# Order of two short GpSimd chains in the last stage of a two-layer gated cross-attention kernel

## The reference, cut to what matters

```python
def expert(w1, bb1, gg1, bbe1, w2, bb2, gg2, bbe2):
    h = relu(layernorm(xf @ w1 + bb1, gg1, bbe1))     # first product
    return layernorm(h @ w2 + bb2, gg2, bbe2)         # second product
...
gate_scores = xf @ gate_W + gate_b                    # top 2 of 4, softmax over the two
out = sum(weights[..., None] * exp_out, axis=1)
x = x + tanh(g_ffn[1]) * (out + xf)                   # xf = layernorm(x)
```

## Time and profile before

| what | value |
|---|---|
| median of 3 runs | 2152.01 us |
| the profiled execution's own time | 2150.5 us |
| its span, first to last instruction | 2148.7 us |
| granted TensorE clock, mean over the span | 0.985 |
| PE busy | 2052.7 us (96%) |
| PEld busy | 1790.2 us (83%) |
| DVE busy | 1762.3 us (82%) |
| ACT busy | 1501.9 us (70%) |
| POOL busy | 1220.5 us (57%) |

### The profile page before, as it was taken

One profiled execution on the slowest core, in us unless ns is written; L12 is line 12 of the kernel. 1 busy time (PEld: TensorE's weight loads), 2 busy tenths in 40 slices (PEclk: granted clock), 3 DMA queues, 4 the chain that ended last, 5 costly groups with the idle time before them and its releaser, 6 DMA issues.

```text
span 2148.7 us, 57822 instructions
## 1 busy us (share of the span) xinstructions
PE 2052.7 (96%) x19788; PEld 1790.2 (83%) x19788; DVE 1762.3 (82%) x4916; ACT 1501.9 (70%) x3234; POOL 1220.5 (57%) x1800
## 2 busy tenths in 40 slices
PE   6999999999699999999699999999899999999997
PEld 5888888888599999999588888888788888888885
DVE  5888888888588888888677777777599999999996
ACT  4766666666487877878366666666577787777785
POOL 5787878887300000000487878777367777777776
PEclk9999999999799999999899999999999999999998
DMA  6555221221466766665322222222101000000000
GB/s 230 188 180 166 64 68 61 70 63 54 158 240 225 248 222 246 223 244 212 135 68 76 72 73 70 71 76 65 41 23 31 31 28 27 30 30 30 30 25 18
DMA packets 151665, 226.12 MB, mean 105 GB/s; under 512 B 20454, under 2 KB 135786, under 8 KB 141036
## 3 DMA queue, kind: packets, MB, share of 16 engines
q1 hardware_dynamic: 145260, 205.99, 28.4%
q0 software_dynamic: 6144, 16.79, 2.6%
HBM read 153.77 MB, written 68.94 MB: 104 GB/s over the span
## 4 chain that ended last, share of the span: by engine, by line
PE 69%; DVE 12%; POOL 6%; issue 6%; DMA 3%; ACT 3%; POOLq 0%; SPq 0%; ACTq 0%; DVEq 0%
PE ps L1254 10%; PE ps L1270 10%; PE ps L1126 10%; PE ps L1111 5%; PE ps L1025 5%; PE ps L1065 4%; PE ps L1202 3%; PE ps L1214 3%; PE ps L1158 3%; DVE k_st L1296 2%; PE ps L984 2%; DMA slots_d<-rows,slot_s 2%; PE ps L1082 2%; POOL k_rs L612 2%; PE ps L1059 2%
## 5 line engine op out<-in xcount | busy, mean ns | idle before, releaser
L1406 DVE TENSOR_REDUCE nmax<-ps 128x16 f32<-128x2048 f32 x128 | 292.3, 2284 | 27.7 <-PE ps L1082 27.4
L873 ACT ACTIVATE prob_t<-ps 128x2048 f32<-128x2048 f32 x128 | 240.9, 1882 | 77.1 <-PE ps L1065 77.1
L688 POOL COPY slot_in<-slot_all 128x1 int32<-128x1 int32 x64 | 11.4, 178 | 472.9 <-DMA eo_d<-eo 472.9
L1025 PE MATMUL ps<-w2f,a_t 128*128 128x256 f32 x1024 | 231.7, 379 | 0.3 <-ACT a_t L805 0.3
L1254 PE MATMUL ps<-xgt_hi,w_hl 128*128 128x256 f32 x1248 | 229.9, 282 | 1.0 <-DVE xgt_lo L1671 1.0
L1270 PE MATMUL ps<-w_hl,hid_hi 128*128 128x256 f32 x1248 | 226.9, 284 | 0.0
L1025 PEld LDWEIGHTS ps<-w2f,a_t 128*128 128x128 f32 x1024 | 189.6, 190 | 23.8 <-ACT a_t L805 0.6
L662 POOL TENSOR_TENSOR km_r<-qk,cst 128x512 fp32r<-128x512 f32 x128 | 133.4, 1042 | 126.7 <-ACT qk L863 126.6
L945 ACT ACTIVATE hid<-ps,b_in 128x256 f32<-128x256 f32 x312 | 145.6, 468 | 82.9 <-PE ps L1254 67.4
L1254 PEld LDWEIGHTS ps<-xgt_hi,w_hl 128*128 128x128 f32 x1248 | 195.3, 189 | 1.4 <-issue 1.4
L805 ACT ACTIVATE a_t<-ps,be_in,g_in 128x128 f32<-128x128 f32 x512 | 185.5, 468 | 12.3 <-PE ps L1044 11.4
(11 more groups left out here) (230 smaller groups left out, 6270.8 us busy)
## 6 DMA issues: line engine op xcount, KB each, us to landing
w_raw<-in_w_dram SPq DMA_DIRECT2D x78, 1024.0 KB, 6.8
c_t<-in_ctx_in_dram SPq DMA_DIRECT2D x128, 128.0 KB
x_d<-x SPq DMA_DIRECT2D x128, 128.0 KB, 2.4
slots_d<-zeros SPq DMA_DIRECT2D x12, 1024.0 KB, 5.9
eo_d<-zeros SPq DMA_DIRECT2D x12, 1024.0 KB, 5.8
xg<-slots_d SPq DMA_DIRECT2D x39, 256.0 KB, 2.7
eo_d<-eo SPq DMA_DIRECT2D x39, 256.0 KB, 2.2
x_in<-in_x_dram SPq DMA_DIRECT2D x64, 128.0 KB, 2.2
```

The costliest lines, as they stand in the source:

```text
L873: nc.scalar.activation(prob_t[:].rearrange("p a k -> p (a k)"), scores.rearrange("p a k -> p (a k)"), ACT.Exp, scale=SOFT).then_inc(y["exp ...
L1025: mm = pe.matmul(dst, a_t[:, b.parity, e, c, :], w2f[:, e, c, :], start=False, stop=True, skip_group_check=True)
L1406: nc.vector.tensor_reduce(nmax[:, b.parity, :, 0:4], scores.rearrange("p a (r k) -> p a r k", k=P), AX_X, ALU.max, negate=True).then_inc(y ...
```

## The change: the row normalisation's chain in front of the second product's chain

In POOL's `fstep` the block for batch s+1 (`frs`, two instructions with their waits) is moved ahead of the block for batch s-2 (`k_rs`, `k_rw`, two instructions with their waits). No instruction is added or removed, and no wait is changed. No other engine's program is changed.

```diff
             def fstep(s):
+                b = s + 1
+                if b.within(B):
+                    st = f["rstd"]
+                    pool.wait_ge(f["st"].of(b), f["st"].at(b))
+                    if (b - 1).begun:
+                        pool.wait_ge(f["xf_done"].of(b - 1), f["xf_done"].at(b - 1))
+                    nc.gpsimd.tensor_tensor(frs[:, 1:2], fmv[:, 1:2], neg_half, ALU.pow).then_inc(st.sem, 1)
+                    pool.wait_ge(st.of(b), st.at(b, 1))
+                    nc.gpsimd.tensor_tensor(frs[:, 3:4], fmv[:, 0:1], frs[:, 1:2], ALU.mult).then_inc(st.sem, 1)
                 b = s - 2
                 if b.within(B):
                     st = f["k_rstd"]
...
                     nc.gpsimd.tensor_tensor(k_rw[:], k_rs[:, 1, :], gw8[:, b.parity, 0:E1], ALU.mult).then_inc(st.sem, 1)
-                b = s + 1
-                if b.within(B):
-                    st = f["rstd"]
-                    pool.wait_ge(f["st"].of(b), f["st"].at(b))
-                    if (b - 1).begun:
-                        pool.wait_ge(f["xf_done"].of(b - 1), f["xf_done"].at(b - 1))
-                    nc.gpsimd.tensor_tensor(frs[:, 1:2], fmv[:, 1:2], neg_half, ALU.pow).then_inc(st.sem, 1)
-                    pool.wait_ge(st.of(b), st.at(b, 1))
-                    nc.gpsimd.tensor_tensor(frs[:, 3:4], fmv[:, 0:1], frs[:, 1:2], ALU.mult).then_inc(st.sem, 1)
                 b = s - 1
```

## The result

The changed kernel took 2126.56 us (median of 4 runs, 2125.72 to 2128.36) against 2151.07 us before (also 4 runs, 2149.14 to 2153.9). The ratio is 0.9886, 95% interval 0.9869 to 0.9903: 24.5 us faster. The forecast was 22 us.

The account below looks back on a forecast made before the run. A circle of waits through `frs` was taken as the bound. 61 x (9.177 - 8.82), rounded 22 us, off 2150.5 gives 2128.5 us, or 2130.0 us from the comparable 2152.0; range 2126 to 2141 us.

Parts of the forecast that it names:

- The circle: Waits through `k_mv`, `k_rs`, `frs`, `xf`, transposes, half the second product and DVE's statistics close once per step, 9.177 us.
- What PE gets: PE: L1008 to L1025 falls from 1.11 to 0.77 us; period without the wait 8.81 us, gaining 22.4 us.
- What is late next: DVE's own period of 8.79 us practically equals PE's 8.81; 8.82 us per step taken, 22 us gained.
- allowance: 8.82 us per step instead of PE's 8.81, as two full engines can't run without ever touching.
- rival A: DVE holds what PE would gain: half of its 0.37 us wait stays, 11 us gained, 2141 us; chance 0.12.
- upper bound: All of PE's 22.4 us and up to 0.8 us at step 2 in the start-up: 23 to 24 us gained.
- `k_rs` and `k_rw` go back: On POOL `k_rw` ends 0.72 us later, costing nothing: 1.2 us of cover is left before ACT's L777.
- B: No change: `xf` is late for another reason, or `frs` now waits for `fmv`; 2152 us, chance 0.04.
- C: Second product's chain late: `k_rw` into ACT's L777, `z`, PE's L1044; 0.82 us per step, 2202 us, chance 0.05.
- D: POOL's `frs` power holds up DVE's short gate-chain instructions: DVE period 9.35 us, 11 us slower, 2163 us; chance 0.03.

Follow-up runs that it names:

- two half-way orders: Against the kernel before: only `frs`'s power ahead of `k_rs`, multiplication behind `k_rw`, 2132.41 us; or both `frs` instructions between `k_rs` and `k_rw`, 2138.67 us.
- first half-way order: Against the kernel before, only the power of `frs` goes ahead of `k_rs`, its multiplication stays behind `k_rw`: 2132.41 us, ratio 0.9911.

## Why the prediction was right, point by point

*The circle.* Right. `frs` held `xf`, `xf` held PE, and `frs` was late only by its place behind `k_rs` and `k_rw`. The run with less PE work in the old order shows that the circle and not PE's work set the step (0.9997). The two half-way orders show that the step follows the delay of `frs` until PE's own period is reached. What the prediction did not see is how close the second way, over POOL's adds, lay behind the one over `k_mv`; the change shortens both, so this did no harm.

*What PE gets.* Right in size: 0.77 us from L1008 to L1025 were taken from the one step that had no wait, and 0.76 were measured. Step without the wait: 8.81 worked out, 8.80 measured. The longer steps of the loop went too, as the prediction said in brackets: before the change some steps per turn took 9.24 to 9.35 us where the others took 9.16, after it all take 8.79 to 8.83.

*What is late next.* Wrong in its number, and so in its ground for an allowance. I took DVE's own period as 8.79 us, from the waits that the list shows (15.9 + 1.2 us in 400). The runs showed 8.56 us: 0.23 us of waiting per step stand in no bracket. DVE was not as good as full, and rival A had nothing to stand on. The two engines were 0.24 us apart and not 0.02, and that the forecast came close all the same is owed to PE's period, which was right, and to an allowance small enough to do no harm: 8.82 instead of PE's 8.81. The forecast's 8.82 is 8.792 in the measurement: 61 x 0.028 = 1.7 us of the 2.5 us that it was short. Of these 0.028 us, 0.019 are the distance to the 8.801 of the other 60 steps, and 0.009 come from the one step from 1 to 2, which takes 8.28. That step gained the 0.79 us of the upper bound, but in all and not on top: 0.38 of it is what every step gained. The rest of the 2.5 us is the scatter between medians and profiled executions.

*`k_rs` and `k_rw` go back.* Right: cost nothing, slack of 1.2 us predicted and 1.24 us measured. One more power of 1.0 us fits in, two don't. One sign came out differently: `k_rs` was to start about 0.9 us after the end of `k_mv` (the prediction's own rows give 1863.98 - 1863.18 = 0.8), and starts 1859.95 - 1859.45 = 0.50 us after it. It has no wait all the same, and nothing was built on the 0.9.

*Rivals.* B fell with ACT's wait for `frs`. C's wait exists, at the predicted place, but only with more than one power of extra delay, and there the step is set by POOL's circle. D as it was put didn't happen: the power of `frs` runs from 1859.17 to 1859.74, and the short instructions of DVE that start in that time take what they took before. Among them are `k_mv`'s L1305, and L1323 (before 139/146/149 ns, now the second line below). L1327 starts only at 1859.74, when the power is over, and is no test of it; it has 211/214/216 ns.

```profile
1859.22 0.23 DVE L1305 TENSOR_SCALAR k_mv<-k_mv,cst 128x4 f32<-128x4 f32 x1
...
L1323 DVE TENSOR_SCALAR gsum<-gexp x46: 140/147/149, 1700.9 to 2096.7; 128x1 f32<-128x1 f32 x46
```

The Trainium skill, "SBUF — State Buffer", section "Who interferes with whom", says that some of VectorE's operations, tensor_scalar among them, and GpSimd's can shut each other out. For POOL's powers, on 1 to 4 elements per partition, no row of these runs shows it. For POOL's adds of 256 elements rows agree with it, and the prediction missed them: it looked at L1327 alone and found no stretch. Once all batches have passed `frs`, in step 63, `k_mv`'s instruction falls into the last add, in the changed kernel (first two lines) and in the one before (from 2119.44, 0.52 us, with the add until 2119.93). It takes 0.53 us instead of 0.23 and ends 0.03 us after the add. With two more powers (last line, the same instruction) it falls into the adds in most steps, and its median is 358 ns, the longest 773:

```profile
2096.01 0.74 POOL L656 TENSOR_TENSOR x<-rest,mixed 128x256 f32<-128x256 f32 x1
...
2096.25 0.53 DVE L1305 TENSOR_SCALAR k_mv<-k_mv,cst 128x4 f32<-128x4 f32 x1
...
L1307 DVE TENSOR_SCALAR k_mv<-k_mv,cst x42: 229/358/773, 1700.4 to 2092.4; 128x4 f32<-128x4 f32 x42
```

In the changed kernel's steps 2 to 62 `k_mv`'s instruction starts as the last add ends or later (1859.22 and 1859.21 in the step shown) and is never stretched, so nothing is paid there. That DVE is held by the add, and not by something else that coincides with it, was not tried by an experiment of its own.

## What to carry to other kernels

Before shortening the engine that looks full, follow the chain of waits once around: if the circle passes through an instruction only because of its place in an in-order queue, a reordering that costs nothing can give more than less work on the full engine (24.5 us against none here). A new order is free as long as what goes back has slack, and the slack can be read as the time from the end of its last instruction to the start of its reader, here 1.24 us; padding of 1.0 us fitted into it and padding of 2.0 us did not. For an engine's own period take a stretch where it had nothing to wait for and not the step less the listed waits, which here left out 0.23 us of 8.79.

## What the runs showed of the hardware that was not expected

The distance from one start to the next tells what short POOL instructions cost. A power on four elements per partition takes 0.98 us to the next instruction if that doesn't read its result (1852.72 to 1853.70, with one more power), and 1.16 us if it does and waits for POOL's own semaphore (1859.95 to 1861.11). For one element it is 0.52 us (1860.91 to 1861.43, in the first half-way order) and 0.64 us (1859.17 to 1859.81). So each link of a chain on POOL costs 0.12 to 0.18 us on top of the work, about as much as a multiplication's whole distance to the next start, 0.14 us (1859.81 to 1859.95).

By the recorded durations a power takes 0.56 us for one element per partition and 1.01 us for four; a multiplication takes 0.19 and 0.20 us. At these sizes the kind of operation counts for more than the number of elements, which costs the power 0.15 us for each further one between these two sizes and the multiplication next to nothing.

A tensor_scalar of DVE on four elements per partition took up to 0.77 us instead of 0.23 where it fell into an add of 256 elements per partition on POOL, and 0.23 us where it fell into a power on POOL (see rival D).
